# Maxima as 64 rows, sums on four column groups, and projections ahead of the value products, in a fused attention layer

## What is computed

```python
x = x + attention(layernorm(x), Wk, Wq, Wv, Wo, bo)   # scores / sqrt(256), softmax over keys
h = layernorm(x)
q, k = heads(h @ Wq), heads(h @ Wk)                   # 8 heads of 64
gl_v = (h @ Ws).reshape(b, t, 8, 5)
wv = topk_mask(gl_v, 2) * sigmoid(gl_v)               # two experts of five
v = einsum('bthe,btek->bhtk', wv, einsum('btd,edk->btek', h, Wv))
probs = softmax(q * 64 ** -0.5 @ k.T)
attn = probs @ v
mask_o = topk_mask((h @ Wd).reshape(b, t, 8, 5), 2)
x = x + einsum('bthe,bthk,ekd->btd', mask_o, attn, Wo)
```

## Time and profile before

| | before |
|---|---|
| median of 3 runs | 5,184.0 us (5,180.48 to 5,186.56) |
| profiled execution | 5,176.93 us, span 5,175.1 us |
| TensorE matmuls (PE) busy | 4,895.9 us, 95% of the span |
| TensorE weight loads (PEld) busy | 2,131.0 us, 41% |
| VectorE (DVE) busy | 3,104.6 us, 60% |
| ScalarE (ACT) busy | 2,355.9 us, 46% |
| GpSimd (POOL) busy | 3,759.7 us, 73% |
| mean granted TensorE clock | 0.933 of full |
| chain that ended last | PE 80%, DVE 12%, POOL 3% |

### The profile page before, as it was taken

The page is one execution under the profiler, slowest core; times in us unless marked ns, Lnnn a source line. Parts: engine busy times, 40 slices in busy tenths (PEclk is TensorE's granted clock), DMA queues, the critical chain, the costliest instruction groups (busy, mean ns, idle before and its releaser), DMA issues.

```text
span 5175.1 us, 63686 instructions
## 1 busy us (share of the span) xinstructions
PE 4895.9 (95%) x23424; PEld 2131.0 (41%) x23424; DVE 3104.6 (60%) x4164; ACT 2355.9 (46%) x3073; POOL 3759.7 (73%) x3149
## 2 busy tenths in 40 slices
PE   5889999999999999999999999999999999999986
PEld 2234444444444444444444444444444444444343
DVE  4566666666666666666666666656666656666431
ACT  2444444444444444444444445444444444444421
POOL 0057777877777777777787777787777787777898
PEclk7799999999999999999999999999999999999987
DMA  3211111111111111111111112111111111111000
GB/s 90 66 51 41 44 51 41 51 45 54 44 42 45 46 45 55 44 41 54 37 48 52 44 41 55 36 51 49 45 44 51 37 54 45 52 44 32 10 5 9
DMA packets 158502, 231.58 MB, mean 45 GB/s; under 512 B 21680, under 2 KB 72688, under 8 KB 158192
## 3 DMA queue, kind: packets, MB, share of 16 engines
q1 hardware_dynamic: 158192, 227.51, 15.4%
HBM read 140.39 MB, written 87.03 MB: 44 GB/s over the span
## 4 chain that ended last, share of the span: by engine, by line
PE 80%; DVE 12%; POOL 3%; ACT 2%; issue 2%; DMA 1%; SPq 0%; POOLq 0%; ACTq 0%; DVEq 0%
PE bank L369 9%; PE ofb L274 9%; PE oab L263 9%; PE expb L223 8%; PE expb L209 6%; PE maxb L239 6%; PE bank L296 5%; PE bank L382 5%; PE maxb L251 4%; PE bank L415 4%; DVE s_mxa L560 4%; PE expb L227 4%; PE bank L349 4%; DVE s_mxf L566 4%; PE bank L329 3%; PE bank L317 2%
## 5 line engine op out<-in xcount | busy, mean ns | idle before, releaser
L560 DVE TENSOR_REDUCE s_mxa<-maxb 128x2 f32<-128x1024 f32 x1024 | 1247.8, 1219 | 348.1 <-PE maxb L239 347.1
L429 ACT ACTIVATE s_pa<-expb 128x1024 f32<-128x1024 f32 x1024 | 1052.8, 1028 | 411.7 <-PE expb L209 399.2
L438 ACT ACTIVATE s_pf<-expb 128x1024 f32<-128x1024 f32 x512 | 524.9, 1025 | 1033.1 <-PE expb L227 1026.4
L566 DVE TENSOR_REDUCE s_mxf<-maxb 128x2 f32<-128x1024 f32 x512 | 627.0, 1225 | 593.5 <-PE maxb L251 592.4
L741 POOL TENSOR_TENSOR s_acc<-s_acc,s_pf 128x512 f32<-128x512 f32 x512 | 661.5, 1313 | 117.6 <-ACT s_pf L438 117.6
L741 POOL TENSOR_TENSOR s_acc<-s_pf 128x512 f32<-128x512 f32 x256 | 320.5, 1274 | 527.7 <-ACT s_pf L438 527.7
L774 POOL TENSOR_TENSOR s_uu<-s_uu,s_pu 128x640 f32<-128x640 f32 x448 | 693.4, 1548 | 11.0
L759 POOL TENSOR_TENSOR s_vh<-s_vh,s_prod 128x512 f32<-128x512 f32 x512 | 652.8, 1275 | 15.5
L263 PE MATMUL oab<-s_pa,s_v 128*17 128x512 f32 x4096 | 614.7, 676 | 0.0
L239 PE MATMUL maxb<-s_ks,s_qs 48*128 48x512 f32 x2048 | 483.3, 457 | 138.0 <-DVE s_mxa L560 97.0
L274 PE MATMUL ofb<-s_pf,s_vh 128*64 128x512 f32 x2048 | 564.0, 629 | 32.0 <-POOL s_vh L759 22.0
(11 more groups left out here) (106 smaller groups left out, 6655.3 us busy)
## 6 DMA issues: line engine op xcount, KB each, us to landing
w_parts<-s_pt SPq DMA_DIRECT2D x128, 512.0 KB, 2.9
s_qs<-w_parts SPq DMA_DIRECT2D x256, 128.0 KB, 3.2
s_ks<-w_parts SPq DMA_DIRECT2D x256, 128.0 KB, 3.1
s_xn<-in_x SPq DMA_DIRECT2D x32, 512.0 KB, 4.7
s_qs<-w_parts SPq DMA_DIRECT2D x256, 64.0 KB, 3.2
s_ks<-w_parts SPq DMA_DIRECT2D x256, 64.0 KB, 3.0
s_xa<-in_x SPq DMA_DIRECT2D x32, 512.0 KB, 4.6
out_y<-s_xa SPq DMA_DIRECT2D x32, 512.0 KB, 2.9
```

What stands on the lines that cost most here:

```text
L429: e.activation(pa[:, k % 3, :, :], xb[:, :, :], ACT.Exp, scale=0.0625).then_inc(a_aexp, 1)
L560: e.tensor_reduce(mxa[:, c, k % 4, 2 * (k // 4):2 * (k // 4) + 2], mb[:, :, :], AX.X, ALU.max, negate=True).then_inc(v_amax, 1)
L566: e.tensor_reduce(mxf[:, pair % 2, i, :], mb[:, :, :], AX.X, ALU.max, negate=True).then_inc(v_fmax, 1)
```

## The change

Three things, and what they need.

The row maxima go to 64 rows: a buffer `mx` of its own, cleared once, gets them in rows 0, 1, 64 and 65; `ones` has ones in the same rows and zeros elsewhere, and the matmul runs over 64 rows.

The sums swap their operands: a 128x32 block of ones is the weights, `acc` moves, 128 columns a matmul, and the four matmuls of a head write four groups of 32 partitions. The result is the sums along the free axis, the same on all 32 partitions of a group, so VectorE transposes 32x32 blocks into `t1` and takes the reciprocal from there.

On TensorE the two products with the values move to the end of their part of the step, behind all projections, transposes and sums. `cg` shares the memory of `prod`, so the comparisons wait for GpSimd's last addition of the batch before.

```diff
-        prod = sb("prod", [128, 4, 2, 64])
+        prod = sb("prod", [128, 640])
+        cg = prod[:, :].rearrange("p (c g) -> p c g", g=64)
+        prod = prod[:, 0:512].rearrange("p (i u k) -> p i u k", i=4, u=2)
-        cg = sb("cg", [128, 10, 64])
-        one = sb("one", [128, 1])
+        one = sb("one", [128, 32])
+        mx = sb("mx", [128, 2, 512], F32R)
...
-                            ra = slice(64 * u, 64 * u + 2)
-                            m = e.matmul(xb[:, u, :], ones[ra, :], mrow[ra, pair % 2, :], start=False, stop=True)
+                            ra = slice(64 * u, 64 * u + 64)
+                            m = e.matmul(xb[:, u, :], ones[ra, :], mx[ra, pair % 2, :], start=False, stop=True)
...
-                    if g == 0 and (r := part_of(s, 1, 16)):
...
-                    if g == 1 and (r := part_of(s, F + 1, 16)):
...
-                            for i in range(4):
-                                m = e.matmul(bk[:, 4 * u + i:4 * u + i + 1], acc[:, u, 128 * i:128 * i + 128], one[:, :],
-                                             start=True, stop=True)
+                            rows = acc[:, u, :].rearrange("p (i q t) -> p q i t", i=4, q=4)
+                            for q in range(4):
+                                m = e.matmul(bk[32 * q:32 * q + 32, 128 * u:128 * u + 128].rearrange(
+                                    "p (i t) -> p i t", i=4), one[:, :], rows[:, q, :, :], start=True, stop=True)
...
+                    if g == 0 and (r := part_of(s, 1, 16)):
...
+                    if g == 1 and (r := part_of(s, F + 1, 16)):
...
-            e.memset(ones[:, :].bitcast(F32), 1.0).then_inc(c_vector, 1)
+            e.memset(ones[:, :].bitcast(F32), 0.0).then_inc(c_vector, 1)
+            e.memset(mx[:, :, :].bitcast(F32), 0.0).then_inc(c_vector, 1)
+            w.wait_ge(c_vector, 4)
+            e.memset(ones[0:2, :].bitcast(F32), 1.0).then_inc(c_vector, 1)
+            e.memset(ones[64:66, :].bitcast(F32), 1.0).then_inc(c_vector, 1)
...
                         w.wait_ge(a_xg, 4 * b + 4)
+                        w.wait_ge(g_val, 36 * b)
...
-                        e.reciprocal(rcf[:, :, :], R.at["sum", b, pair][:, 0:8].rearrange("p (u i) -> p u i", u=2)
+                        e.transpose(t1[:, 0, 0:256], R.at["sum", b, pair][:, 0:256]).then_inc(v_sum, 1)
+                        w.wait_ge(v_sum, 2 * n + 1)
+                        e.reciprocal(rcf[:, :, :], t1[:, 0, 0:256].rearrange("p (u i t) -> p u i t", u=2, t=32)[:, :, :, 0]
                                      ).then_inc(v_sum, 1)
...
-                            e.dma_start(mrow[64 * u:64 * u + 2, pair % 2, :].bitcast(F32), maxf[pair][:, u, :]
+                            e.dma_start(mx[64 * u:64 * u + 2, pair % 2, :].bitcast(F32), maxf[pair][:, u, :]
```

More of the change, by code:

```diff
@@ L374, in tensor @@
                         n = 4 * b + pair
-                        bk, before = R.next(("sum", b, pair), v_sum, n + 1)
+                        bk, before = R.next(("sum", b, pair), v_sum, 2 * n + 1)
                         if before:
@@ L417, in tensor @@
                         m.then_inc(p_y, 1)
+                    if g == 0 and (r := part_of(s, 1, 16)):
+                        b, n = r
+                        j, kc = n // 4, n % 4
+                        w.wait_ge(a_aexp, 32 * b + 2 * n + 2)
+                        w.wait_ge(a_v, 2 * b + 2)
+                        if kc == 0:
+                            w.wait_ge(c_vector, 7)
+                            w.wait_ge(v_tr, 4 * b + j)
+                        for h in range(4):
+                            m = e.matmul(oa[32 * h:32 * h + 17, :], v32[:, b % 2, kc, 4 * j + h, :],
+                                         pa[:, (32 * b + 2 * n + h // 2) % 3, h % 2, :], start=(kc == 0), stop=(kc == 3))
+                        m.then_inc(p_apv, 1)
+                    if g == 1 and (r := part_of(s, F + 1, 16)):
+                        b, n = r
+                        pair, kc = n // 4, n % 4
+                        w.wait_ge(a_fexp, 16 * b + n + 1)
+                        w.wait_ge(g_val, 36 * b + 9 * pair + 9)
+                        if kc == 0:
+                            w.wait_ge(a_osb, 4 * b + pair)
+                        for u in range(2):
+                            m = e.matmul(of[64 * u:64 * u + 64, :], vh[:, kc, 2 * pair + u, :],
+                                         pf[:, (16 * b + n) % 3, u, :], start=(kc == 0), stop=(kc == 3))
+                        m.then_inc(p_fpv, 1)
         def scalar(e):
@@ L747, in gpsimd @@
                         if n == 0 or n % 2 == 1:
-                            to = vv if n == 0 else prod[:, :, :, :]
+                            to = vv if n == 0 else prod
                             w.wait_ge(v_gate, NG * b + NG)
@@ L758, in gpsimd @@
                             w.wait_ge(g_val, k)
-                            e.tensor_tensor(vv, vv, prod[:, :, :, :], ALU.add).then_inc(g_val, 1)
+                            e.tensor_tensor(vv, vv, prod, ALU.add).then_inc(g_val, 1)
                     for pair in range(4):
@@ L802, in sync @@
                 e.dma_start(dst, src).then_inc(c_weights, 16)
-            w.wait_ge(c_vector, 4)
+            w.wait_ge(c_vector, 7)
             for s in SLOTS:
```

25 lines of the change are left out of this document (2 added, 23 removed).

## The result

The changed kernel takes **4,760.64 us** (median of 4 runs, 4,756.67 to 4,762.58), the kernel before 5,182.24 us in the runs beside it: a ratio of **0.9186, with a 95% interval of 0.917 to 0.9202**. The profiled execution took 4,762.58 us, with a span of 4,760.8 us.

The account below looks back on a forecast made before the run. TensorE, 98% busy, was taken to bound the kernel. Gains of 205, 163 and 108 us less 29 make 447: from the profiled 5,176.9 us to 4,730, plus 7 for the median, rounded to 4,740 us; range 4,660 to 4,890.

Parts of the forecast that it names:

- 64 rows: TensorE's row maxima in the array form of their neighbours: three gaps shrink, 0.40 us in each of 512 steps, 205 us.
- sums: TensorE's sums on four column groups with overlapping records: 0.60 us a block instead of 1.87, 128 times, 163 us.
- clock: TensorE's falls to the lower clock go if the sums cause them: 328 us at 0.33 is 108 us.
- order: Projections, transposes and sums ahead of the products with the values on TensorE: nothing, with 16 us either way.
- VectorE at the gates: Where the gates are computed, VectorE can't pass on all of TensorE's gain: 0.9 us a batch lost, -29 us.
- The rival of sums without overlap: The sums' records run one after the other at 0.117 us: 163 us missing, 4,903 us; chance 0.08.
- The one in which each column group pays 0.30 for emptying the array: Each of 16 sum records pays 0.30 us, sums take 4.8 us, falls stay: 5,354 us; chance 0.03.
- The rival in which the falls stay: Transposes after the sums, or the next waits, lower the clock, so 108 us stay: 4,848 us; chance 0.12.
- the rival's 2.9: VectorE passes on nothing more around the gates: 2.9 us a batch lost instead of 0.9, about 4,810 us; chance 0.12.
- the 3 us named as the limit: Sign of being wrong: TensorE's waits for VectorE's maxima grow by over 3 us a batch.
- GpSimd: Gated values of the first pair stay ready before the products using them: of 0.85 us margin some 0.4 stay.
- The shared buffer: Gate comparisons wait for GpSimd's last addition of the batch before; 25 us between them cover it, so no cost.

Follow-up runs that it names:

- two_rows: The changed kernel with the maxima's matmul over 2 rows again instead of 64: 4,949.37 us, ratio 0.9557 to the kernel before.
- y_behind: The changed kernel with only the output projection put behind the two products with the values again: 4,746.39 us, ratio 0.9153 to the kernel before.
- sums_alone: The kernel before with only the new sums and VectorE's transpose of them, old order and two-row maxima: 4,927.44 us, ratio 0.952.
- one_column_sums: The changed kernel with the old sums of one moving column and without VectorE's transpose of them: 4,962.49 us, ratio 0.958 to the kernel before.
- no_transpose: The changed kernel without VectorE's new transpose of the sums, so most rows get another row's sum: 4,767.52 us, ratio 0.9197 to the kernel before.
- gates_spread: y_behind with VectorE's pieces of the ranks at the gates moved to other places: 4,720.53 us, ratio 0.9107 to the kernel before.

## Why the prediction was right

Per batch, what the runs give for its three gains comes to 6.56 (maxima), 5.2 (sums) and 4.3 (clock), 16.0 us in all. 13.29 arrived, so 2.7 us are missing, where 0.9 were allowed for. Times 31 batches:

| step of the prediction | predicted, us | measured, us | from |
|---|---|---|---|
| 64 rows | 205 | 203 | 16 parts x 0.41; two_rows costs 189 |
| sums | 163 | 161 | 4 x 1.30; block of 0.58, predicted 0.60 |
| clock | 108 | 132 | 13.4 us less at the lower level a batch, x 0.32 |
| order | 0 | -17 | y_behind, 0.54 a batch |
| VectorE at the gates | -29 | -68 | what is left of 13.29; 50 of it at the gates |
| sum | 447 | 411 | |

*64 rows* was right in mechanism and size: a gap belongs to the change of form between neighbours.

*Sums*: right in both. The rival of sums without overlap falls with the L363 group. The one in which each column group pays 0.30 for emptying the array falls as well: sixteen records take 0.58 us.

*Clock.* The price per us was right: the parts of the kernel before with a fall, set against the same parts without, lost 4.45 us a batch in 13.94 us at the lower level, 0.32. (Part 2 of step 1 and part 0 of step 2 have a fall in every batch; they are set against sums_alone.) The term was too small because it counted only the 328 us read from a rounded mean over 500 to 4,600 us: that stretch holds 362 us, and 31 batches at 13.4 us make 414. Over the whole span the kernel before stands at the lower level for 693 us, the changed one for 247. The cause was only partly right. The change of the sums alone removes 277 of 328 us, but one_column_sums keeps the old sums and has hardly a fall behind them. Old sums with two-row products give 328 us, or 392 in the new order; old sums with 64 rows keep 184 in the old order, and in the new one next to nothing outside step 14. The rival in which the falls stay is out: the transposes stand at the same place in the changed kernel and in sums_alone, and 14 and 51 of 328 us are left. In the kernel before, 37 of the 65 falls begin before the transposes that follow the sums. The Trainium skill ("TensorE: Matmul & The Clock Gate", "Part 4: PE-mode transpose") says that transposes don't count as activity in the way that matmuls do; whether they have a share in the falls of step 14 no run shows, since none takes them out.

*Order* was set at nothing, within 16 us, and that bound was wrong. As a part of this change it gains 36 us beside the other two, and alone it costs 77. The gain is inside the row of the gates in this table, since it comes mostly there. The -17 is the output projection, which loses its overlap with the next scores; y_behind gets 14 us back, and no step of the prediction looked at it.

*VectorE at the gates* is the term that was mis-sized: 0.9 us a batch, and 2.2 are missing beside the 0.54 of the projection. 1.3 of them lie between the start of part 2 of step 13 and the end of step 14, and 0.3 in part 2 of step 12. These 1.6 are at the gates, where the prediction looked, and within its bound of 2.1 and short of the rival's 2.9. The other 0.6 lie in part 2 of step 0, where it didn't look: there L254 waits for a maximum that VectorE takes behind its transpose and combination of the first attention's products (L605 to L613). VectorE there in order of time, then TensorE, in one such place:

```profile
1689.06 0.71 DVE L605 STREAM_TRANSPOSE s_t<-oab 128x512 f32<-128x512 f32 x1
...
1690.09 0.72 DVE L613 TENSOR_TENSOR s_comb<-s_t,s_rca 128x256 f32<-128x256 f32 x1
1690.74 1.21 DVE L568 TENSOR_REDUCE s_mxa<-maxb 128x2 f32<-128x1024 f32 x1
...
1692.01 0.50 PE L254 MATMUL maxb<-s_hi 64*128 64x512 f32 x2 [0.16 <-DVE s_mxa L568]
```

The prediction asked what VectorE could pass on within one stretch, and gave no price to the parts behind it. What it named as the added load, the transpose, isn't what decides (no_transpose gains nothing). Where the pieces of the gates stand does: gates_spread gets 26 us back. That the clock's 24 us too little and the gates' 39 too much partly cancel is luck. The recorded waits for maxima grew by 36 us, 1.2 us a batch, within the 3 us named as the limit.

*GpSimd* kept its margin. Its last product for a first pair and the block that uses it (second attention, L419), in order of time, answering to the earlier trace rows:

```profile
2119.53 1.27 POOL L770 TENSOR_TENSOR s_vh<-s_vh,s_prod 128x512 f32<-128x512 f32 x1
...
2121.95 1.08 PE L419 MATMUL ofb<-s_pf,s_vh 128*64 128x512 f32 x4
```

1.15 us are left, 0.4 predicted, with the sums in front as foreseen. *The shared buffer* costs nothing: the comparisons that use it (L645) have 0.1 us of idle time in front of them in the whole run.

## What to carry to other kernels

Give neighbouring matmuls one array form, with zeros in the rows that aren't needed: here that gained 0.4 us a pair at no cost. Let a matrix whose partitions are summed go through as moving columns behind a narrow block of ones, in column groups, instead of as weights for one column: here 0.58 us instead of 1.87. After each such gain ask where the next engine's hand-placed pieces stand, and move them: what was hidden when TensorE was slower turns up as waits, and here most of the clock's falls that were left stood behind long waits gathered in one place.

## What had not been expected of the hardware

**The clock's falls have no single cause.** Behind the same 1.88 us of old sums the clock falls in every batch in one step and never in another, and changing the order moves it from steps 1 and 2 to steps 9 and 10. The rows show two kinds of falls. In the kernel before, all 65 begin beside the sums, with no idle time of TensorE over 0.04 us in the 8 us ahead. In the changed kernel all four begin some 9 us behind the sums and behind a wait of 1.3 us in step 14. Such a wait doesn't always bring one: y_behind has the same waits in step 14, 2.4 us a batch, and no fall there in 24 batches. The longest of them in order of time, in y_behind:

```profile
2091.71 0.50 PE L242 MATMUL maxb<-s_ks,s_qs 48*128 48x512 f32 x2 [1.28 <-DVE s_mxa L568]
```

Which sequences bring a fall stays open; no run here isolates it.

**VectorE waits out GpSimd's instruction.** VectorE and GpSimd (POOL) in order of time, in the changed kernel at the ranks:

```profile
2091.20 2.50 POOL L752 TENSOR_TENSOR s_acc<-s_pf 128x512 f32<-128x512 f32 x2 [9.54 <-ACT s_pf L442]
...
2092.48 1.30 DVE L661 TENSOR_TENSOR s_rk<-s_rk,s_prod 128x64 f32<-128x64 f32 x1
2093.71 0.21 DVE L662 TENSOR_TENSOR s_rk<-s_prod,s_sk 128x64 f32<-128x64 f32 x1
```

L661 and L662 are the same operation on 64 columns. The first takes 1.30 us and ends at 2093.78, just behind GpSimd's second addition (2093.70); the next takes 0.21. Of 32 such L661, 30 are longer than 0.7 us, and all 30 end within 0.15 us of the end of a GpSimd instruction. With the pieces elsewhere (gates_spread) L661 takes 0.22 us on average. The Trainium skill ("SBUF — State Buffer", "SBUF: two separate sides") describes this as a lock on a shared port that is held for a whole instruction; the trace agrees. It is why a piece of the gates has no fixed price: the first ranks (L650) went from 0.35 to 1.13 us on average when moved, and the 25 long ones of 32 all end 0.2 us behind a GpSimd instruction.
